# TensorE's loop turned behind the first P@V of a batch row, and the last batch row's down products in halves over four steps

## The reference, cut to what matters

```python
xn = layernorm(x)                                  # over the 256 channels
q, k, v = split(xn @ qkv_w + qkv_b)                # 16 heads of 16 channels
attn = softmax(q @ k.T * 16 ** -0.5)               # 512 x 512 for each head
out  = (attn @ v) @ proj_w + proj_b
gate = xn @ w_gate.T / 127;  up = xn @ w_up.T / 127  # hidden size 768, integer weights
ffn  = (silu(gate) * up) @ w_down.T / 127
x = x + out + ffn
```

## Time and profile before

| | us |
|---|---|
| median of the three timed runs | 574.96 |
| the profiled execution, its own time | 576.71 |
| its span, first to last instruction | 574.9 |
| TensorE busy | 555.6 (97%) |
| VectorE busy | 464.9 (81%) |
| ScalarE busy | 418.0 (73%) |
| GpSimd busy | 305.1 (53%) |

### The profile page before, as it was taken

The page is one execution under the profiler, slowest core; times in us unless marked ns, Lnnn a source line. Parts: engine busy times, 40 slices in busy tenths (PEclk is TensorE's granted clock), DMA queues, the critical chain, the costliest instruction groups (busy, mean ns, idle before and its releaser), DMA issues.

```text
span 574.9 us, 13815 instructions
## 1 busy us (share of the span) xinstructions
PE 555.6 (97%) x4844; PEld 334.2 (58%) x4844; DVE 464.9 (81%) x601; ACT 418.0 (73%) x573; POOL 305.1 (53%) x286
## 2 busy tenths in 40 slices
PE   7898899999999999999999999999999999998896
PEld 6656456565655557556665656555665556554453
DVE  5797777888878888888878889888978888788732
ACT  3666865888668975888668875788758886787572
POOL 3283536755564745755566554846467555355120
PEclk9899989999999999999999999999999999999999
DMA  8896086363854368371872449371873438520101
GB/s 235 254 244 146 3 216 179 57 141 118 236 110 105 62 198 206 56 164 71 245 143 69 98 156 241 62 156 29 228 189 61 93 138 227 99 57 21 57 2 38
DMA packets 55119, 74.89 MB, mean 130 GB/s; under 512 B 5680, under 2 KB 28208, under 8 KB 55088
## 3 DMA queue, kind: packets, MB, share of 16 engines
q1 hardware_dynamic: 55088, 74.47, 52.0%
HBM read 40.90 MB, written 33.03 MB: 129 GB/s over the span
## 4 chain that ended last, share of the span: by engine, by line
PE 90%; DVE 4%; ACT 3%; issue 1%; DMA 1%; SPq 0%; ACTq 0%
PE dense L1280 23%; PE o_bank L1254 22%; PE st_bank L1221 16%; PE dense L1324 14%; PE s_bank L1238 11%; PE dense L1264 2%; DVE neg_max L1004 1%; ACT probs L841 1%; PE dense L1393 1%; DMA probs<-in_L_attn_qkv_w 1%; PE dense L1380 0%; DVE w_dl L1033 0%; PE s_bank L1221 0%; ACT w_qkvh L830 0%; ACT probs L927 0%
## 5 line engine op out<-in xcount | busy, mean ns | idle before, releaser
L1004 DVE TENSOR_REDUCE neg_max<-s_bank 128x2 f32<-128x1024 f32 x250 | 304.9, 1220 | 73.9 <-PE s_bank L1238 72.8
L841 ACT ACTIVATE probs<-st_bank 128x1024 f32<-128x1024 f32 x250 | 256.4, 1026 | 112.6 <-PE st_bank L1221 109.4
L1254 PE MATMUL o_bank<-probs,v_ones 128*32 128x512 f32 x1024 | 137.1, 607 | 0.1
L1221 PEld LDWEIGHTS st_bank<-q_stack,k_stack 50*128 50x128 f32 x500 | 47.7, 184 | 131.7 <-ACT probs L841 82.1
L1221 PE MATMUL st_bank<-q_stack,k_stack 50*128 50x512 f32 x500 | 118.0, 466 | 5.3 <-ACT probs L841 5.0
L1238 PE MATMUL s_bank<-k_stack,q_stack 48*128 48x512 f32 x500 | 108.9, 429 | 0.9 <-DVE neg_max L1004 0.7
L742 POOL TENSOR_TENSOR hid_tl<-gated,hid_th 128x512 fp32r<-128x512 f32 x48 | 61.7, 1285 | 35.2 <-ACT hid_th L941 35.2
L736 POOL TENSOR_TENSOR gated<-gated,hid 128x512 f32<-128x512 f32 x48 | 61.7, 1285 | 28.7 <-DVE gated L1026 19.8
L1280 PE MATMUL dense<-xn_tl,w_gh 64*128 64x512 f32 x176 | 61.9, 391 | 0.0
L1280 PE MATMUL dense<-xn_tl,w_uh 64*128 64x512 f32 x176 | 61.9, 391 | 0.0
L1238 PEld LDWEIGHTS s_bank<-k_stack,q_stack 48*128 48x128 f32 x500 | 47.4, 185 | 20.7 <-DVE neg_max L1004 8.4
(11 more groups left out here) (152 smaller groups left out, 886.2 us busy)
## 6 DMA issues: line engine op xcount, KB each, us to landing
q_stack<-q_spread SPq DMA_DIRECT2D x64, 192.0 KB, 4.7
k_stack<-k_spread SPq DMA_DIRECT2D x64, 192.0 KB, 5.2
q_spread<-qk_parts SPq DMA_DIRECT2D x16, 512.0 KB, 3.8
k_spread<-qk_parts SPq DMA_DIRECT2D x16, 512.0 KB, 3.5
q_spread<-qk_parts SPq DMA_DIRECT2D x16, 256.0 KB, 4.1
k_spread<-qk_parts SPq DMA_DIRECT2D x16, 256.0 KB, 2.0
resid<-in_L_attn_x SPq DMA_DIRECT2D x16, 256.0 KB, 4.3
out<-resid SPq DMA_DIRECT2D x15, 256.0 KB, 2.2
```

The costliest lines, as they stand in the source:

```text
L841: nc.scalar.activation(probs[:, s % 2, 2 * half:2 * half + 2, :], transposed_bank(row, s, half)[:, :, :], ACT.Exp, scale=SCALE).then_inc(e ...
L1004: nc.vector.tensor_reduce(neg_max[:, g % 2, :, NT * pair + qt], score_bank(row, half)[:, :, :], AX_X, ALU.max, negate=True).then_inc(max_d ...
L1221: done = nc.tensor.matmul(transposed_bank(row, s, half)[:, r, :], k_stack[rows, pair, P * kt:P * (kt + 1)], q_stack[rows, pair, :], start= ...
L1254: done = nc.tensor.matmul(o_bank[32 * j:32 * (j + 1), :], v_ones[:, kt, 8 * (g // 2) + 2 * j + g % 2, :], probs[:, (s - 1) % 2, j, :], sta ...
```

## The change

TensorE's loop body used to begin at step 0 of a batch row. Now the part of step 0 up to and including its P@V (`until_probs_v`) of batch row 1 stands ahead of the loop; the body runs from behind that P@V (`from_probs_v`) to behind the P@V of step 0 of the next batch row. The order of the matmuls in batch rows 0 to 6 is the same; the loop's counter and branch move from behind the last `scores` of step 15 to behind the P@V of step 0.

The eighth batch row gets its own table `LAST`. The second `proj` moves from step 6 to step 4; the down products are listed at steps 6 and 8 (before: 9 and 10), and their second stretch comes behind `scores(s,1)` instead of around `scores_t(s,0)`. So each of the four stretches of 24 matmuls lies in a step of its own, steps 6 to 9. ScalarE copies each finished down product into `hid` (`leave_down`) and GpSimd adds it to the residual (`add_down`), in place of VectorE's addition. On SyncE the second `store` and `load_resid` of this batch row come ahead of `load_max` 2.

```diff
+LAST = [
...
+    (3, 0, "proj", 0, -1, (2, 1)),
+    (4, 0, "proj", 1, -1, (2, 0)),
+    (6, 0, "max", 2, 0, (0,)), (6, 0, "down", 0, 0, (1, 2)),
+    (8, 0, "down", 1, 0, (1, 2)),
...
+DOWN_ADDED_AT = ((8, 1), (10, 1))
...
+def over_two_steps(like, kind):
+    return like == ROWS - 1 and kind == "down"
...
+                if row.like == ROWS - 1:
+                    store(row, 1)
...
+                if row.like == ROWS - 1:
+                    load_resid(row, 1)
...
+            def add_down(row, i):
+                pool.wait_ge(act_free, count(row, freed_by_act, kind="down", index=i))
+                pool.wait_ge(resid_ready, NT * row.at + 2 * i + 2)
+                both = resid[:, 2 * i:2 * i + 2, :]
+                nc.gpsimd.tensor_tensor(both, hid[:, i, :].rearrange("p (t c) -> p t c", t=2), both, ALU.add
+                                        ).then_inc(down_added, 1)
...
+            def leave_down(row, chunk):
+                act.wait_ge(dense_done, count(row, any_chunk, chunk))
+                nc.scalar.activation(halves(hid[:, chunk[3], :]), bank_of(chunk), ACT.Copy).then_inc(act_free, 1)
...
+                        for chunk in chunks_at(row, s - 1, slot):
+                            if over_two_steps(row.like, chunk[2]):
+                                leave_down(row, chunk)
...
-                dve.wait_ge(dve_free, count(Row(ROWS - 1, ROWS - 1), freed_by_dve, kind="down", index=1))
+                dve.wait_ge(down_added, KC)
...
-                            if chunk[2] == "down":
+                            if chunk[2] == "down" and not over_two_steps(row.like, chunk[2]):
...
+            def behind_probs_v(row, s, exact):
+                carried = carried_at(row, s)
+                chunks(row, s, 1, exact)
+                if row.has(0) and not after_scores(row, s):
+                    scores_t(row, s, 1)
+                ahead = product_at(row, s + 1)
+                if pair_ahead(row, s, 1):
+                    scores(row, s, 1)
+                if carried:
+                    end_product(row, carried, exact, 2)
+                if ahead:
+                    begin_product(row, ahead, exact)
+                chunks(row, s, 2, exact)
...
+            def from_probs_v(row, exact):
+                behind_probs_v(row, 0, exact)
+                for s in range(1, STEPS):
+                    until_probs_v(row, s, exact)
+                    behind_probs_v(row, s, exact)
...
                 step(Row(0, 0), exact)
+                until_probs_v(Row(1, 1), 0, exact)
                 with pe.Fori(1, ROWS - 2) as b:
-                    step(Row(b, 1), exact)
-                step(Row(ROWS - 2, ROWS - 2), exact)
+                    from_probs_v(Row(b, 1), exact)
+                    until_probs_v(Row(b + 1, 2), 0, exact)
+                from_probs_v(Row(ROWS - 2, ROWS - 2), exact)
                 step(Row(ROWS - 1, ROWS - 1), exact)
```

More of the change, by code:

```diff
@@ L86 @@
 ]
+LAST = [
+    (0, 0, "up", 4, 0, (2,)), (0, 0, "gate", 4, 0, (0,)),
+    (1, 0, "v", 1, 0, (1, 2)),
+    (2, 0, "up", 5, 0, (1,)), (2, 0, "gate", 5, 0, (0,)), (2, 0, "max", 1, 0, (2,)),
+    (3, 0, "proj", 0, -1, (2, 1)),
+    (4, 0, "proj", 1, -1, (2, 0)),
+    (6, 0, "max", 2, 0, (0,)), (6, 0, "down", 0, 0, (1, 2)),
+    (8, 0, "down", 1, 0, (1, 2)),
+    (10, 0, "max", 3, 0, (0,)),
+]
+DOWN_ADDED_AT = ((8, 1), (10, 1))
 ENDS = {"up": (0, 1)}
@@ L123, in in_parts @@
     return like >= 0 and (kind, i) in IN_PARTS
+def over_two_steps(like, kind):
+    return like == ROWS - 1 and kind == "down"
 def freed_by_act(like, kind, i):
-    return kind in ("v", "up") or like >= 0 and kind in ("q", "k", "proj")
+    return kind in ("v", "up") or over_two_steps(like, kind) or like >= 0 and kind in ("q", "k", "proj")
 def freed_by_dve(like, kind, i):
@@ L183, in chunks_of @@
         return FIRST
+    if like == ROWS - 1:
+        return LAST
     return [c for c in STEADY if 0 <= like + c[4] < ROWS and not (like == ROWS and c[2] == "proj")]
@@ L397, in build @@
         hid_low = sem("hid_low")
+        down_added = sem("down_added")
         half_made = sem("half_made")
@@ L663, in step @@
                     load_max(row, 2)
-                if row.has(0) and row.has(-1):
+                if row.has(0) and row.has(-1) and row.has(1):
                     store(row, 1)
@@ L670, in step @@
                     load_later_weights()
-                if row.has(0):
+                if row.has(0) and row.has(1):
                     load_resid(row, 1)
@@ L802, in step @@
                                                         ALU.add).then_inc(resid_ready, 1)
+                        if row.like == ROWS - 1 and (s, slot) in DOWN_ADDED_AT:
+                            add_down(row, DOWN_ADDED_AT.index((s, slot)))
                         if left_at(row, s, slot, DIVIDE):
@@ L1504, in product_at, with carried_at, until_probs_v @@
                 return found[0] if found else None
+            def carried_at(row, s):
+                here = product_at(row, s)
+                return here if here and over_two_steps(row.like, here[2]) else None
+            def until_probs_v(row, s, exact):
+                if row.like == -1:
+                    chunks(row, s, 0, exact)
+                here = product_at(row, s)
+                carried = carried_at(row, s)
+                if carried:
+                    here = None
+                if here and s == 0:
+                    begin_product(row, here, exact)
+                if here:
+                    end_product(row, here, exact, 0)
+                if row.has(0):
+                    scores_t(row, s, 0)
+                if here:
+                    end_product(row, here, exact, 1)
+                if pair_ahead(row, s, 0):
+                    scores(row, s, 0)
+                if here:
+                    end_product(row, here, exact, 2)
+                if row.has(0):
+                    chunks(row, s, 0, exact)
+                if after_scores(row, s):
+                    scores_t(row, s, 1)
+                if row.like == ROWS and s == 0:
+                    project_first_half()
+                if 0 < STEPS * row.like + s <= STEPS * ROWS:
+                    probs_v(row, s)
+                    if row.like == ROWS:
+                        stay_busy(BUSY_AFTER_LAST)
+                        project_last_half()
@@ L1506, in step @@
             def step(row, exact):
                 for s in range(STEPS):
-                    if row.like == -1:
-                        chunks(row, s, 0, exact)
-                    here = product_at(row, s)
-                    if here and s == 0:
-                        begin_product(row, here, exact)
-                    if here:
-                        end_product(row, here, exact, 0)
-                    if row.has(0):
-                        scores_t(row, s, 0)
-                    if here:
-                        end_product(row, here, exact, 1)
@@ L1519, in step @@
-                    if pair_ahead(row, s, 0):
-                        scores(row, s, 0)
-                    if here:
-                        end_product(row, here, exact, 2)
-                    if row.has(0):
-                        chunks(row, s, 0, exact)
-                    if after_scores(row, s):
-                        scores_t(row, s, 1)
-                    if row.like == ROWS and s == 0:
-                        project_first_half()
-                    if 0 < STEPS * row.like + s <= STEPS * ROWS:
-                        probs_v(row, s)
-                        if row.like == ROWS:
-                            stay_busy(BUSY_AFTER_LAST)
-                            project_last_half()
@@ L1535, in step @@
-                    chunks(row, s, 1, exact)
-                    if row.has(0) and not after_scores(row, s):
-                        scores_t(row, s, 1)
-                    ahead = product_at(row, s + 1)
-                    if pair_ahead(row, s, 1):
-                        scores(row, s, 1)
-                    if ahead:
-                        begin_product(row, ahead, exact)
-                    chunks(row, s, 2, exact)
+                    until_probs_v(row, s, exact)
+                    behind_probs_v(row, s, exact)
```

2 lines of the change are left out of this document (added).

## The result

The changed kernel takes 571.13 us in the median (570.33 to 571.64) against 574.91 for the kernel before beside it: a ratio of 0.993 with a 95% interval of 0.9913 to 0.9948. The forecast was 571.9 in 570.7 to 573.8.

The account below looks back on a forecast made before the run. TensorE, busy 97% of the span, was taken to set the end, with its standing still in step 0 and the eighth batch row. Gains 1.0 + 2.1 = 3.1 us: 574.96 - 3.1 = 571.9, range 570.7 to 573.8.

Parts of the forecast that it names:

- The loop, forecast 1.0: Step 0 of batch rows 1 to 5: moving counter and branch behind P@V(0) saves 0.96 plus 0.07, written 1.0 us.
- I take the full difference: 4 x (4.56 - 4.32): Step 0 at four back edges falls to the written-out step's 4.32 us, saving 0.96 us.
- under 1.0 us of P@V: Behind P@V(0): branch and first threshold, 0.26 us more than without a jump, are hidden while the P@V streams.
- The eighth batch row, forecast 2.1: Its steps 4 to 10 fall from 29.04 to 26.82 us; less a 0.1 charge, 2.1 us gained (0.8 to 3.1).
- step 5's 0.2 for the addition: Eighth batch row, step 5: VectorE's addition for the moved `proj` mostly fits between reductions; 0.2 us added, window 3.83.
- VectorE loses two additions: Eighth batch row: a clause noting VectorE no longer adds the down products; no gain of its own was assigned.
- The charge of 0.1 for the last maxima: Behind step 10, eighth batch row: ScalarE's copy of the maxima may stand behind an exponential, 0 to 0.6 us; 0.1 charged.
- steps 11 to 15 further apart: Sign of being wrong: these steps' P@Vs further apart would show gain spent on ScalarE's exponentials or the last maxima.
- The branch's cost: Rival, chance 0.12: the branch's cost moves along, step 0 stays near 4.55, only the batch row's 2.1 remain: 572.9 us.
- the halves fit: Negates a rival, chance 0.12: half down products push scores late, windows near 4.07, gain 1.8 in all: 573.2 us.
- both parts came through: Negates a rival, chance 0.08: loop and eighth batch row both at their lower bounds, 0.3 us gained: 574.7.
- the slower rival: Four back edges each wait for an instruction fetch, 4 x 1.7 = 6.8 us against 2.1 gained: 579.7; chance 0.04.

Follow-up runs that it names:

- the whole products: Changed kernel with each down product of the eighth batch row whole again, in steps 6 and 8; executed once: steps 4 to 10 sum to 28.70 us.
- the turn alone: Changed kernel with the loop turned but the eighth batch row's table of before; ratio 0.9985 (0.9975 to 0.9995) to the kernel before.

## Why the prediction came out

**The loop, forecast 1.0, measured 1.5 to 1.6.** The direction, the place and the sign (`scores_t(0,1)` 0.99 behind P@V(0)) are right. The step that was mis-sized is "I take the full difference: 4 x (4.56 - 4.32)": the floor is not the written-out 4.32 but 4.21, as the order of waits has it, and batch row 6, for which I had counted nothing, now has the loop's form as well (4.32 to 4.21). By rows, 4 x 0.34 + 0.11 + 0.08. The reason I gave, that the branch lies "under 1.0 us of P@V", is wrong in its place: by the runs with the edge ahead of the P@V and behind the score it is the stream's lead that counts. The row of L1233 showed that lead, and I read it as a lead under the P@V only. So the loop's term outran the upper end that I had given it.

**The eighth batch row, forecast 2.1, measured 2.9 less 0.06.** TensorE's standing still in steps 7 and 8 was the right thing to look at, and the whole products show that it was the bulk. Windows forecast and measured: 3.61 and 3.72, 3.83 and 3.53, 4.09 and 3.95, 3.74 and 3.55, 3.81 and 3.71, 3.81 and 3.72, 3.93 and 3.94. The largest miss is step 5's 0.2 for the addition: by its window, VectorE takes it in the gap (busy for 3.53 of 3.53 us) and TensorE loses nothing. In steps 8 and 9 I had the scores 1.48 behind the P@V; the rows have 1.40 (538.60, 537.20), since the score product ahead is shorter there:

```profile
536.87 0.40 PE L1280 MATMUL s_bank<-k_stack,q_stack 48*128 48x512 f32 x2
537.31 1.23 DVE L1046 TENSOR_REDUCE neg_max<-s_bank 128x2 f32<-128x1024 f32 x1 [0.67 <-PE s_bank L1280]
538.60 0.50 PE L1280 MATMUL s_bank<-k_stack,q_stack 48*128 48x512 f32 x2
538.93 0.87 PE L1322 MATMUL dense<-w_dh,hid_th 64*128 64x256 f32 x12
```

The reduction starts 0.44 behind a product of 0.40 us, not 0.54 as behind one of 0.50. In step 7 the half follows the score by 0.23, not 0.34, and the score comes 0.07 earlier.

**What I had costed at nothing.** For ScalarE's copies and GpSimd's additions no wait of TensorE is listed, and in step 8, where the first of each stands (538.1 and 538.7), TensorE is busy throughout; that they cost nothing, as forecast, is read from this alone. But "VectorE loses two additions" was worth more than a clause: 1.5 us of the gain hang on it. The charge of 0.1 for the last maxima was 0.06 to 0.07: one of my signs of being wrong, steps 11 to 15 further apart, did come, at the size I had charged.

**The total.** 4.35 between the P@Vs and 3.8 in the median, against 3.1: both terms were too small. The 4.35 lie beyond 1.0 + 3.1 = 4.1, the upper ends from which the range was made, so that the median fell into the range is in part luck: it was 571.13 in the first set, but 570.10 and 570.26 in the other two, under the range's lower end of 570.7.

**The rivals.** The branch's cost did not move with it, the halves fit, both parts came through. The jump still takes 208 ns, so no wait for instructions shows at a back edge. But I wrote that no row has the duration of such a fetch, and the trace of before may hold one: the line of the `If` around the two copies of the batch rows, 70 ns where it falls through at 46.3 us and 3601 where it jumps over the other copy at 570.0:

```profile
L1562 PEldq COMPARE_BRANCH  x2: 70/1836/3601, 46.3 to 570.0; - x2
```

It ends at 573.6, before the span does (574.9), and costs nothing there. That it waits for instructions fits the Trainium skill ("Runtime: NRT & Kernel Launch", section Instruction fetch mechanics), which has a jump out of the held window wait for a DMA; no run here took the jump apart. At this price the slower rival would have been dearer, about 4 x 3 us, and no likelier.

## What to carry to other kernels

A loop's edge costs what TensorE's stream has no lead for: put it where several products are already handed on, not behind one that waits for another engine. Before a window is called the floor, look whether its waits are in a good order: where two stand ahead of one instruction, the one that ends last should not be the one that becomes, or stands ahead of, an instruction of its own. In the written-out code and in step 12 it had to be written first here, in step 0 of the loop second; the trace says which. And when work is spread into the gaps of one engine, count as well who frees the banks that it writes into.

## What was not expected of the hardware

In some executions TensorE's granted clock falls to its lower level for some 3 us in step 7 of batch row 0, with no difference in the program. In two other profiles, of the whole down products and of the loop written out, it fell near the end instead, as told above. The windows from 73 to 76 us of the kernel before and of the turn alone (the last three columns are the granted clock, the DMA share and GB/s):

```profile
73.00:76.00 3.00, 3.00 (x15) 1.22 (x16) 1.29 (x2) 1.46 (x4) 1.27 (x1) 0.55 0.97 315
```

```profile
73.00:76.00 3.00, 3.00 (x25) 1.71 (x27) 2.46 (x3) 2.14 (x4) 1.63 (x2) 1.00 0.92 317
```

The changed kernel has 0.50 there, which is 1.2 of 2.4 GHz. The step takes 5.1 us then and 3.6 otherwise, though in the 10 us from 60 to 70 TensorE was busy for 9.1 to 10.0 at the full clock, with the drop and without. Of the three profiles of the changed kernel two have it and one has not, so it is chance; at 1.5 us a time it is as large as a part of this change, and it is why the verdicts above rest on windows.
